# A Mamba and MLP kernel: the first chunk's time step in two halves, and the weight loads behind the first rows of B

## What is computed

```python
x_and_res = x @ W_in.T;  xp, res = split(x_and_res)
xc = silu(causal_conv4(xp) + conv_b)
ssm = xc @ W_x.T                       # B (16), C (16), dt (1)
dt = softplus(dt @ W_dt.T + b_dt)      # the time step, one per inner channel
h = exp(A * dt) * h + dt * B * xc      # over time, for each of 16 states
y = sum(h * C) + D * xc;  return silu(y + res) @ W_out.T
...
x = x + mamba(layernorm(x));  x = x + ternary_mlp(layernorm(x))
```

## Time and profile before

| what | us |
|---|---|
| median of 3 runs | 2729.62 (2729.12 to 2730.76) |
| the profiled execution | 2731.1 |
| its span, from the first to the last instruction | 2729.4 |
| TensorE, weight loads, busy | 2554.4, 2339.7 |
| VectorE, ScalarE, GpSimd busy | 2339.9, 2219.9, 2166.2 |

### The profile page before, as it was taken

How to read it: one execution, slowest core, us unless ns; L and a number is a source line. 1 busy time by engine, 2 the same in 40 slices (tenths; PEclk the granted TensorE clock), 3 DMA queues, 4 the chain that set the end, 5 groups by cost and what they waited for, 6 DMA issues and landing times.

```text
span 2729.4 us, 52680 instructions
## 1 busy us (share of the span) xinstructions
PE 2554.4 (94%) x18562; PEld 2339.7 (86%) x18562; DVE 2339.9 (86%) x2767; ACT 2219.9 (81%) x4560; POOL 2166.2 (79%) x1696
## 2 busy tenths in 40 slices
PE   6679999999999999999999999999987999999999
PEld 5558888888888888888888888888877999999999
DVE  4999999999999999999999999999994277777776
ACT  7898888888888888888888888888877677777774
POOL 3788888888888888888888888888885576676763
PEclk8889999999999999999999999999989999999999
DMA  6112211211221122221121112121232222222220
GB/s 235 43 45 67 67 59 59 71 59 59 63 63 60 63 65 66 64 74 63 59 65 65 59 59 67 59 62 60 67 132 66 78 78 94 94 94 94 93 94 33
DMA packets 130187, 199.01 MB, mean 73 GB/s; under 512 B 16384, under 2 KB 93312, under 8 KB 129920
## 3 DMA queue, kind: packets, MB, share of 16 engines
q1 hardware_dynamic: 129920, 195.57, 22.2%
HBM read 144.68 MB, written 50.86 MB: 72 GB/s over the span
## 4 chain that ended last, share of the span: by engine, by line
PE 63%; DVE 18%; issue 9%; ACT 4%; POOL 1%; DVEq 1%; ACTq 0%; POOLq 0%
PE banks L1735 17%; PE banks L1770 15%; PE banks L1747 11%; DVE h L1401 9%; PE banks L1647 7%; DVE acc L1414 5%; PE banks L1799 5%; PE banks L1698 4%; DVE silu L1386 3%; PE banks L1721 2%; PE banks L1658 2%; ACT banks L1203 1%; PE banks L1689 1%; PE banks L1711 1%; DVEq L1400 0%
## 5 line engine op out<-in xcount | busy, mean ns | idle before, releaser
L1401 DVE TENSOR_TENSOR_SCAN h<-banks,ub 128x512 f32<-128x512 f32 x1024 | 1198.7, 1211 | 41.1 <-ACT banks L1203 34.3
L872 POOL TENSOR_TENSOR ub<-u,b_row 128x1020 f32<-128x1020 f32 x512 | 1216.1, 2375 | 0.3 <-issue 0.2
L1414 DVE SCALAR_TENSOR_TENSOR acc<-banks,c_tok,acc 128x512 f32<-128x512 f32 x1024 | 721.2, 741 | 75.8 <-PE banks L1747 75.4
L1203 ACT ACTIVATE banks<-dt,neg_a 128x510 f32<-128x510 f32 x1024 | 698.9, 688 | 67.1 <-DVE h L1401 66.2
L1747 PE MATMUL banks<-ident,h 128*128 128x128 f32 x4096 | 597.9, 278 | 101.2 <-DVE acc L1414 64.8
L1747 PEld LDWEIGHTS banks<-ident,h 128*128 128x128 f32 x4096 | 478.8, 142 | 190.0 <-DVE h L1401 109.0
L1735 PE MATMUL banks<-act_high,h_rounded 128*128 128x256 f32 x2048 | 516.3, 291 | 8.4 <-POOL act_low L899 6.7
L1735 PE MATMUL banks<-act_low,h_rounded 128*128 128x256 f32 x2048 | 496.3, 281 | 0.0
L1735 PEld LDWEIGHTS banks<-act_high,h_rounded 128*128 128x128 f32 x2048 | 388.6, 190 | 15.1 <-issue 14.5
L1735 PEld LDWEIGHTS banks<-act_low,h_rounded 128*128 128x128 f32 x2048 | 389.0, 190 | 0.1
L871 POOL TENSOR_TENSOR ub<-b_u,enter 128x4 f32<-128x4 f32 x512 | 105.9, 207 | 261.3 <-DVE h L1401 252.6
(11 more groups left out here) (157 smaller groups left out, 5519.4 us busy)
## 6 DMA issues: line engine op xcount, KB each, us to landing
b_row<-b_scratch SPq DMA_DIRECT2D x128, 512.0 KB, 4.0
z_scratch<-z_out SPq DMA_DIRECT2D x128, 256.0 KB, 2.1
zl_raw<-z_scratch SPq DMA_DIRECT2D x32, 1024.0 KB, 7.2
x_sb<-in_x SPq DMA_DIRECT2D x32, 256.0 KB, 4.3
x_res<-in_x SPq DMA_DIRECT2D x32, 256.0 KB, 3.3
h_full<-in_h SPq DMA_DIRECT2D x2, 4096.0 KB, 18.2
x_scratch<-x_sb SPq DMA_DIRECT2D x32, 256.0 KB, 2.8
out_e<-x_scratch SPq DMA_DIRECT2D x16, 512.0 KB, 3.9
```

Of the source, the lines that this page charges most:

```text
L872: nc.gpsimd.tensor_tensor(ub[:, n % 2, :, 1:], u[:, :, 1:], b_row[:, n // QUARTER % 2, n % QUARTER:n % QUARTER + 1, 1:].to_broadcast([P, E ...
L1203: nc.scalar.activation(decay_half(k)[:, :, 1:], dt[:, par, 2 * i:2 * i + 2, 1:], ACT.Exp, scale=neg_a[:, n:n + 1]).then_inc(decay_ready, 1)
L1401: nc.vector.tensor_tensor_scan(h[:, n % 2, 2 * i:2 * i + 2].rearrange("p e t -> p (e t)"), banks[:, k % DECAYS, :], ub[:, n % 2, 2 * i:2 * ...
L1414: nc.vector.scalar_tensor_tensor(out=acc[:, par, q], in0=turned[q], scalar=c_tok[:, par, q, n:n + 1], in1=acc[:, par, q], op0=ALU.mult, op ...
```

## The change

For chunk 0 a new function `soft_first` makes the time step on ScalarE two tiles at a time: Abs of both, Exp over both, Relu of both, Ln over both, then the same for the other two. VectorE adds and multiplies a half as soon as its Ln is done. Two new semaphores, `first_soft` and `first_dt`, carry this. The psum bank of the time step is given free behind the last Ln instead of behind the last Relu. Later chunks keep the old way. On SP the loads of w1, w2 and h1 move behind `write_b(0)` and the two `read_b`. The early checks move from steps 1 to 6 to steps 5 to 10 of chunk 0, the three late ones from steps 7 to 9 to steps 11 to 13.

```diff
-        CHECK_AT = [(0, 1 + k // 2) for k in range(EARLY)] + [(0, 7 + k) for k in range(3)] + [(1, k) for k in range(LATE - 3)]
+        CHECK_AT = [(0, 5 + k // 2) for k in range(EARLY)] + [(0, 11 + k) for k in range(3)] + [(1, k) for k in range(LATE - 3)]
...
             load_x(1)
-            for name, src in (("w1", w1), ("w2", w2), ("h1", h1)):
-                sp.dma_start(full[name][:], src.rearrange("(k p) n -> p k n", p=P)).then_inc(early_in, 16)
             write_b(0)
             read_b(0, 0)
             read_b(0, 1)
+            for name, src in (("w1", w1), ("w2", w2), ("h1", h1)):
+                sp.dma_start(full[name][:], src.rearrange("(k p) n -> p k n", p=P)).then_inc(early_in, 16)
             load_x(2)
...
+            def soft_first():
+
+                rows = bank("dtc", 0)
+                for half in range(2):
+                    tiles = range(ET // 2 * half, ET // 2 * (half + 1))
+                    part = soft[:, ET // 2 * half:ET // 2 * (half + 1)]
+                    for e in tiles:
+                        last = nc.scalar.activation(soft[:, e], rows[:, 0:T], ACT.Abs, scale=w_dt_sb[:, e:e + 1], bias=b_dt_sb[:, e:e + 1])
+                    last.then_inc(first_soft, 1)
+                    act.wait_ge(first_soft, 4 * half + 1)
+                    nc.scalar.activation(part, part, ACT.Exp, scale=-1.0).then_inc(first_soft, 1)
+                    for e in tiles:
+                        last = nc.scalar.activation(dt[:, 0, e], rows[:, 0:T], ACT.Relu, scale=w_dt_sb[:, e:e + 1], bias=b_dt_sb[:, e:e + 1])
+                    last.then_inc(first_soft, 1)
+                    act.wait_ge(first_soft, 4 * half + 2)
+                    nc.scalar.activation(part, part, ACT.Ln, bias=1.0).then_inc(first_soft, 1)
+                act.wait_ge(first_soft, 8)
+                act.sem_inc(freed("dtc", 0), 1)
+                act.sem_inc(soft_step, 3)
...
                     nc.scalar.activation(c_tok[:, par], rows[:, T:].rearrange("p (n r) -> p n r", n=NT)[:, :, ROW_C:ROW_C + NS], ACT.Copy)
+                    if c == 0:
+                        soft_first()
+                        return
...
                 if c == 0 and n == 0:
-                    wait_taken(dve, "dtc", 0)
-                    dve.wait_ge(soft_step, 3)
-                    nc.vector.tensor_tensor(dt[:, 0], dt[:, 0], soft[:], ALU.add).then_inc(dt_ready, 1)
-                    dve.wait_ge(dt_ready, 1)
                     for j in range(2):
                         wait_taken(dve, f"conv{j}", 0)
-                    nc.vector.tensor_tensor(u[:], dt[:, 0], xc[:], ALU.mult).then_inc(u_ready, 1)
+                    for half in range(2):
+                        tiles = slice(ET // 2 * half, ET // 2 * (half + 1))
+                        dve.wait_ge(first_soft, 4 * (half + 1))
+                        nc.vector.tensor_tensor(dt[:, 0, tiles], dt[:, 0, tiles], soft[:, tiles], ALU.add).then_inc(first_dt if half == 0 else dt_ready, 1)
+                        dve.wait_ge(first_dt if half == 0 else dt_ready, 1)
+                        last = nc.vector.tensor_tensor(u[:, tiles], dt[:, 0, tiles], xc[:, tiles], ALU.mult)
+                    last.then_inc(u_ready, 1)
```

More of the change, by code:

```diff
@@ L246, in program @@
         soft_step = sem("soft_step")
+        first_soft = sem("first_soft")
+        first_dt = sem("first_dt")
         dt_ready = sem("dt_ready")
@@ L1072, in front @@
                     last.then_inc(soft_step, 1)
-                if n == ACT_AT["z"] + 1:
+                if n == ACT_AT["z"] + 1 and c >= 1:
                     rows = bank("dtc", c)
@@ L1078, in front @@
                     last.then_inc(freed("dtc", c), 1)
-                if n == ACT_AT["z"] + 2:
+                if n == ACT_AT["z"] + 2 and c >= 1:
                     act.wait_ge(soft_step, 3 * c + 1)
                     nc.scalar.activation(soft[:], soft[:], ACT.Exp, scale=-1.0).then_inc(soft_step, 1)
-                if n == ACT_AT["soft"]:
+                if n == ACT_AT["soft"] and c >= 1:
                     log_soft(c)
```

## The result

The changed kernel took 2740.55 us (median of six runs, 2737.32 to 2740.97), the kernel before on the same chip 2730.19. The ratio is 1.0034, with an interval of 1.0024 to 1.0044: 9.3 us slower, 6.6 to 12.0. (The ratio is estimated from all the runs and isn't the quotient of the two medians, which differ by 10.4 us.) Against the 2729.62 us that the prediction started from, that is 2738.9: slower as forecast, 2.6 us above the 2736.3, within the range of 2731.0 to 2739.5.

A forecast was written before the change was run, and what follows sets the result against it. The chain was 63% TensorE and 18% VectorE, but the edit acts only in chunk 0's first 107 us. Step 11's +6.7 us on the profiled 2731.1 gave 2737.8, or 2736.3 us for the median (1.5 lower); range 2731.0 to 2739.5.

The forecast's parts named there:

- Halves: Chunk 0's time step before the scan: product u ends at 35.5 against 36.01, a gain of 0.5 us.
- B's rows: SP in chunk 0: goes on at 28.3 instead of 31.46; first scan near 38.9, 1.4 us earlier.
- Landing of x: x of chunk 2, queued behind w1, w2 and h1: lands at 51.8 us, upper bound 53.6.
- Who waits: ScalarE in step 2 stands from about 42 to 51.8 for x; scan 2b comes at 54.7 instead of 48.32.
- Steps 3 to 5: Chunk 0: VectorE paces, lower TensorE clock adds up to 0.7 us; decay 5b at 64.5 to 65.1, +0.8 to +1.4.
- Steps 5 to 10: Chunk 0, ScalarE without idle time: five more checks cost 6.0 us; step 11 comes 6.1 to 6.7 us later.
- One to one from step 11: From step 11 of chunk 0 VectorE paces as before, so the shift, taken as +6.7 us, carries to the end.
- A: Step 2 of chunk 0: x isn't late, step 11 at 83.9, -2.7 us, total 2726.9; chance 12%.
- B: x of chunk 2 lands later still, at h2's pace: +8.5 to +9.0 us, total 2738.4; chance 10%.
- C: Chunks 1 to 3: part of the loss is made good later, 0 to +4 us, total 2732; chance 10%.
- D: Start of chunk 0: B's rows aren't earlier, as three large loads follow closely; total as forecast, no chance of its own.
- the clock term: Steps 3 to 5 of chunk 0: TensorE's convolution at the lower clock after idling adds up to 0.7 us.

The follow-up runs named there:

- the spread checks: Changed kernel with its 15 checks of chunk 0 in steps 6 to 8 and 11 to 15, x of chunk 2 still late: 2737.02 us, 1.0020 of before.

## Where the prediction was right and where it was off

- **Halves.** u at 35.10, forecast 35.5. The 512-column passes took 0.53 from start to start (28.60 to 29.13), the lower end, not 0.61; the gain was 0.8, not 0.5. Being behind a wait, it changed nothing.
- **B's rows.** Issue 28.20 (28.3), first scan 38.58 (38.9). Right.
- **Landing of x: the mis-sized term.** ScalarE began on it at 53.73, forecast 51.8: +1.9, a shade above my upper bound of 53.6. The order was right, the pace was not. I took the 15.3 us in which w1, w2 and h1 had drained; there nothing large was queued behind them. Here h2 stood right behind x, the engines moved 410 GB/s all the time (first stretch above), and h1 landed 11.6 us after w2: 4.19 MB in 11.6 us is 361 GB/s. About an eighth of the traffic was thus something else, and the likeliest is h2; no run isolates it. The row of h2's own pace, which I had as bound, had a load behind it too and was the nearer one. The Trainium skill ("DMA: Bandwidth & Descriptors", "Where 436 GB/s comes from") has HBM bind at about 358 GB/s for a core, and by it x would have landed at 54.1, an estimate. That time is nearly right, but the reason is not borne out, since the engines moved 410 in total; the measurement decides. The Trainium skill (the same page, "Queues, rings and completion order") says that each engine consumes its ring in order; the 21.5 us of x behind 6 MB agree.
- **Who waits.** ScalarE at the sums of x, 11.42 us idle where I had about 10, scan 2b at 56.60 (54.7): the 1.9 carried on. The 1.4 us gained were swallowed.
- **Steps 3 to 5.** SiLU's table load at 62.36 is the forecast's 60.3 and 1.9, and 0.1; decay 5b at 66.64, within 64.5 to 65.1 plus 1.9. The visit took 66.64 - 62.36 = 4.28 against 63.73 - 59.55 = 4.18: of the 0.7 us that I gave to TensorE's lower clock 0.1 was seen there. The clock was at 0.50, as I said, but it showed on VectorE's adds (0.99 and 0.51 in step 3), which were not last in this kernel; with the spread checks they were.
- **Steps 5 to 10.** From decay 5b to the carry behind Ln 93.88 - 66.64 = 27.24 us, before 84.95 - 63.73 = 21.22: +6.0, as forecast for the five more checks. Step 11 at +8.29 is then my +6.7, with 1.9 more for x and 0.6 less for the clock, and 0.3 left over.
- **One to one from step 11: not quite.** 0.7 us came in steps 11 to 15 and 0.4 in chunk 1, where I had nothing. An add of step 13 waited 0.59 for TensorE, whose granted clock still was 0.55 from 100 to 104 us; before, in the stretch that lies 8.3 earlier (92 to 96), it was 0.79. The late checks themselves cost nothing, as said.
- **Rivals.** A (x not late) would have needed x by 43.5; it landed ten later. With x put first by hand, its step 11 of 83.9 was met within 0.6 (84.45), and its total, 2.7 below before, lies in the interval of that run. B (x later still, at h2's pace) is what happened to x; I had given it 10%, and its 2738.4 lies half a microsecond from the 2738.9, which is above the forecast's own range of 2734.5 to 2738.5. C and D left no trace.
- **What would show it.** Of the signs of being wrong one came: the first scan of chunk 1 was 8.99 us late, not about 6.7.

The forecast of sign, place and mechanism was right. It fell 2.6 us short: 1.9 for one row chosen too kindly, 1.1 behind step 11 where it had no term, and 0.3 unexplained, against which the clock term, 0.6 too high, helped by luck.

## What to carry to other kernels

Where a load is moved, read what stands behind it in the same queue: it was the next small transfer that paid here, not the one that was moved for. To price a transfer behind large ones, take a row in which large ones are also queued behind it. A gain ahead of a wait is worth nothing until the wait is gone, and a work item moved off a busy stretch is only free if it doesn't land ahead of the first instruction of the next stage.

## What the hardware showed that was not expected

SP's issue instructions themselves take long when much is queued: x of 256 KB 5.48 us and w3 of 1 MB 10.07 us in the changed kernel, 11.05 for w3 with x first, against 0.43 for x and 0.50 for h2 in the earlier trace rows, and 1.60 for w3 in that kernel. Since SP works in order, everything behind is issued late as well: the third quarter of B at 50.2 us in both kernels, hidden in one by the late scan, a wait of 7.78 us in the other.

A wait on one engine was followed by a lower clock of another: behind ScalarE's wait TensorE had no matmul for 9.20 us, up to 57.23, and its granted clock was 0.55 from 52 to 56 us and 0.50 in the next stretch, in which it was busy for 2.77 of 4 us. Eight matmuls of the convolution took 3.75 us there, against 1.97 in the kernel before, where the granted clock was 1.00 from 50 to 54 us.
